# Weighted sum of the expert rows on VectorE: four operations over four token tiles in place of eight over one

## What is computed

```python
x = x + 0.5 * ffn(layernorm(x))
x = x + attn(layernorm(x))
x = x + 0.5 * ffn(layernorm(x))

def ffn(x):                     # 8 experts, the 2 best of each token
    gates = softmax(x @ gate_w)
    top_v, top_i = top_k(gates, 2)
    top_v = top_v / sum(top_v)
    eo = gelu(x @ fc_w[e]) @ proj_w[e]          # for every expert e
    return sum over the two choices c of top_v[c] * eo[top_i[c]]
```

## Time and profile before

| what | us |
|---|---|
| median of 3 runs | 1348.94 |
| range of the runs | 1347.59 to 1349.1 |
| profiled execution | 1347.8 |
| its span in the profile | 1346.0 |
| VectorE busy | 840.0 (62%) |
| GpSimd busy | 650.5 (48%) |
| TensorE busy | 1029.9 (77%) |
| busy time of L824, 96 instructions | 40.8 |

### The profile page before, as it was taken

The page is one execution under the profiler, slowest core; times in us unless marked ns, Lnnn a source line. Parts: engine busy times, 40 slices in busy tenths (PEclk is TensorE's granted clock), DMA queues, the critical chain, the costliest instruction groups (busy, mean ns, idle before and its releaser), DMA issues.

```text
span 1346.0 us, 23815 instructions
## 1 busy us (share of the span) xinstructions
PE 1029.9 (77%) x7084; PEld 899.3 (67%) x7084; DVE 840.0 (62%) x2514; ACT 722.3 (54%) x1804; POOL 650.5 (48%) x473
## 2 busy tenths in 40 slices
PE   1428788750899999999999999999999706878870
PEld 1427777740787778878778778877887606777770
DVE  4662222227888887888888888888887493222226
ACT  1102222211888888888889889888898201222220
POOL 1146777743353444434444444444444044777772
PEclk9988999985999999999999999999999658999995
DMA  7896555541000000000000000000000203555545
GB/s 207 116 167 197 147 152 156 151 132 54 1 2 1 1 1 1 2 1 1 1 1 1 1 1 1 1 1 1 1 1 1 63 0 115 154 149 153 152 111 187
DMA packets 61065, 87.13 MB, mean 65 GB/s; under 512 B 8019, under 2 KB 32598, under 8 KB 60944
## 3 DMA queue, kind: packets, MB, share of 16 engines
q1 hardware_dynamic: 51200, 66.08, 18.9%
q0 software_dynamic: 9744, 19.56, 4.9%
HBM read 65.67 MB, written 20.97 MB: 64 GB/s over the span
## 4 chain that ended last, share of the span: by engine, by line
PE 47%; DVE 22%; DMA 10%; issue 9%; POOL 9%; ACT 1%; DVEq 1%; another core or an unknown queue 0%; SPq 0%; POOLq 0%; ACTq 0%
PE bank L1046 8%; DMA xr<-xn_dram,gidx 7%; PE bank L1020 6%; DVE qst L857 6%; PE bank L1036 6%; PE bank L1037 5%; POOL y_dram L504 5%; PE bank L1058 4%; PE bank L1056 4%; DVE prob L879 3%; PE bank L976 3%; POOL xr L498 3%; PE bank L986 3%; DVE x_sb L824 2%; DVE in_tile L753 2%
## 5 line engine op out<-in xcount | busy, mean ns | idle before, releaser
L536 POOL TENSOR_TENSOR prob<-prob,rsum 128x512 f32<-128x512 f32 (+3 forms) x128 | 296.1, 2321 | 381.5 <-DVE rsum L886 381.5
L600 ACT ACTIVATE prob<-prob,negmax 128x384 f32<-128x384 f32 (+3 forms) x512 | 283.2, 556 | 25.9 <-DVE negmax L879 24.2
L879 DVE CUSTOM_DVE_ANT_0 prob<-bank,bias_tab 128x384 f32<-128x384 f32 (+3 forms) x512 | 243.1, 489 | 70.8 <-PE bank L1037 60.2
L578 ACT ACTIVATE hT<-bank 128x512 f32<-128x512 f32 x144 | 86.0, 597 | 372.6 <-PE bank L976 372.6
L891 DVE TENSOR_TENSOR pl<-bank,ph 128x512 fp32r<-128x512 f32 x320 | 219.9, 687 | 26.0 <-ACT ph L609 22.4
L1036 PE MATMUL bank<-kst,qst 128*128 128x256 f32 (+2 forms) x512 | 182.6, 371 | 23.3 <-DVE qst L857 21.0
L609 ACT ACTIVATE ph<-bank 128x512 fp32r<-128x512 f32 x320 | 188.8, 590 | 19.6 <-PE bank L1046 17.3
L1046 PE MATMUL bank<-ident,prob 128*128 128x128 f32 x1280 | 193.7, 274 | 0.7 <-POOL prob L536 0.6
L1046 PEld LDWEIGHTS bank<-ident,prob 128*128 128x128 f32 x1280 | 156.8, 140 | 48.1 <-POOL prob L536 10.2
L815 DVE COPY yo<-bank 128x128 f32<-128x128 f32 x144 | 42.0, 292 | 214.1 <-PE bank L986 209.9
L498 POOL DMA_INDIRECT xr<-xn_dram,gidx x144 | 140.1, 973 | 72.8 <-issue 31.1
(11 more groups left out here) (152 smaller groups left out, 1366.9 us busy)
## 6 DMA issues: line engine op xcount, KB each, us to landing
w1t<-L_ffn_fc_w SPq DMA_DIRECT2D x144, 256.0 KB
in_tile<-y_dram SPq DMA_DIRECT2D x16, 512.0 KB, 4.3
bias_dram<-hg SPq DMA_DIRECT2D x1, 5120.0 KB, 52.9
xn_dram<-in_tile SPq DMA_DIRECT2D x8, 512.0 KB, 2.9
bias_tab<-bias_dram SPq DMA_DIRECT2D x1, 4096.0 KB, 13.0
xr<-xn_dram,gidx POOLq DMA_INDIRECT x144
y_dram<-yo,sidx POOLq DMA_INDIRECT x144
x_sb<-L_attn_x SPq DMA_DIRECT2D x4, 512.0 KB, 7.9
```

The source lines that it names most:

```text
L536: g.tensor_tensor(out=pv, in0=pv, in1=rsum[:, n % 4, :].unsqueeze(2).to_broadcast([P, HG, (n % QT + 1) * P]), op=ALU.mult).then_inc(norm_d ...
L600: a.activation(prob[n % QT][:, h, :], prob[n % QT][:, h, :], ACT.Exp, scale=-1.0, bias=negmax[:, (HG * n + h) % 8:(HG * n + h) % 8 + 1], a ...
L879: v.tensor_tensor_reduce(out=prob[n % QT][:, h, :], in0=front[:, 0:w], in1=bias_tab[:, HG * (n // QT) + h, SEQ - w:SEQ], scale=-1.0, scala ...
```

## The change

The loop is unrolled, and a group is now four `tensor_tensor` instructions of 128x512 in place of eight `scalar_tensor_tensor` of 128x128. The first two multiply the rows of both choices in their buffer by the weights, which are read with a step of zero along the features. The third adds the first product to x, the fourth the second. The fourth waits for the third and for the second multiplication. It raises `combined` by four at once, which is what SyncE's waits count on.

```diff
-                with dve.Fori(0, TILES // 16) as i:
+                for i in range(TILES // 16):
                     for u in range(3):
-                        dve.wait_ge(y2_in[u], (i + (r * (TILES // 16) + 1)) * 16)
+                        done = (r * (TILES // 16) + i) * 9 + 3 * u
+                        own = slice(i * 16 + u * 4, i * 16 + u * 4 + 4)
+                        dve.wait_ge(y2_in[u], (r * (TILES // 16) + i + 1) * 16)
                         for c, w in ((0, gw1), (1, gw2)):
-                            for q in range(4):
-                                t = i * 16 + (u * 4 + q)
-                                xt = x_sb[:, ds(t, 1), :].rearrange("p a d -> p (a d)")
-                                v.scalar_tensor_tensor(out=xt, in0=yc[:, u, q, c * D:(c + 1) * D], scalar=w[:, ds(t, 1)],
-                                                       in1=xt, op0=ALU.mult, op1=ALU.add).then_inc(comb1 if c == 0 else combined, 1)
-                            if c == 0:
-                                dve.wait_ge(comb1, i * 12 + (r * (TILES * 3 // 4) + (u + 1) * 4))
+                            part = yc[:, u, :, c * D:(c + 1) * D]
+                            v.tensor_tensor(part, part, w[:, own].unsqueeze(2).to_broadcast([P, 4, D]), ALU.mult).then_inc(comb1, 1)
+                        dve.wait_ge(comb1, done + 1)
+                        v.tensor_tensor(x_sb[:, own, :], x_sb[:, own, :], yc[:, u, :, 0:D], ALU.add).then_inc(comb1, 1)
+                        dve.wait_ge(comb1, done + 3)
+                        v.tensor_tensor(x_sb[:, own, :], x_sb[:, own, :], yc[:, u, :, D:2 * D], ALU.add).then_inc(combined, 4)
```

## The result

The changed kernel takes 1353.36 us (median of 9 runs), the kernel before 1348.87 in the same comparison. The ratio is 1.0033 with a 95% interval of 1.0018 to 1.0047: it is slower by 4.5 us, 2.4 to 6.3. One of the nine runs took 1597.42 us at a granted clock of 0.655, and the ratio leaves it out. The forecast was 1351.3 with a range of 1348.2 to 1354.2. The time lies in the range, but the ratio is above the limit of 0.2% (2.7 us) under which I had put the larger chance.

A forecast was written before the change was run, and what follows sets the result against it. VectorE and its hold-ups by GpSimd were taken to bound both combine stages, about 21 us each. First stage +1.6 and second +0.8 gave +2.4 us on 1348.94: 1351.3 us, range 1348.2 to 1354.2.

The forecast's parts named there:

- An undisturbed group costs 0.28 us more: Combine stages: a VectorE group not meeting GpSimd's work takes 2.59 us in place of 2.31.
- Rival B: Combine stages: each wide VectorE operation must end before the next starts, giving 1353.9 us; chance 0.18.
- Turns of whole operations: Combine stages: VectorE and GpSimd alternate one whole operation each; GpSimd's lengthen from 1.07 and 1.26 to 1.4 and 1.6 us.
- Rival A: Combine stages: GpSimd isn't delayed, its chain stays 4.8 us, both stages stay within 0.3 us: 1348.9; chance 0.18.
- rival C: Combine stages: the new form doesn't collide and both engines run side by side, faster at 1344.3 us; chance 0.07.
- First stage, +1.6: First combine stage: GpSimd's second chain ends last, so the statistics start at 320.65 in place of 319.09.
- Second stage, +0.8: Second combine stage: GpSimd's chain ends at 1341.0, so the second output transfer goes later; +0.9, taken as +0.8 us.
- The sum: Both combine stages together: +2.4 us on the kernel before's median of 1348.94.
- the outer part of the forecast's bounds: Share of the forecast's own chance, 0.22 of 0.57, put beyond the 0.2% (2.7 us) limit; its bounds were +0.8 and +4.6.
- a GpSimd start that overlaps nothing: Upper bound, both stages: GpSimd's start can't overlap VectorE's turn, six or seven turns cost 0.17 more each; total +4.6 us.
- The loop's branch and register work: Combine loop: unrolling removes this work, but no gap at the loop's turn is on record, so worth 0.
- My sign that something outside the sum was at work: Attention, between the stages: a length change of over 1 us would make the sum wrong for an outside reason.

The follow-up runs named there:

- E5: Changed kernel with both products written to PSUM, so the additions read only one SBUF input; ratio 0.9989 to the kernel before, 1.5 us faster.
- E6: Changed kernel with products and weights both in PSUM, so no VectorE operation of the stage has two SBUF inputs; ratio 0.9968, 4.3 us faster than before.
- E8: Kernel before, unrolled, with a group's running sum in PSUM, so the second four operations read one SBUF input; ratio 0.9982, 2.4 us faster.
- E1: The changed kernel run again without edit, on another chip; ratio 1.0026 to the kernel before, 3.7 us on 1431.96.
- E2: Kernel before with only the loop unrolled, its eight 128x128 operations a group kept; ratio 0.9985, 2.1 us faster.
- E3: Kernel before with GpSimd's operations cut from 128 features to 1, leaving out most of its sums; ratio 0.9893, 15.3 us faster.
- E4: Changed kernel with GpSimd's operations cut from 128 features to 1; ratio 0.9926 to the kernel before, 10.6 us faster.
- E9: Changed kernel with GpSimd's rows brought first; ratio 1.0011 to the kernel before, 1.6 us slower, interval reaching to no change.
- E12: As E6, with GpSimd's rows brought first; ratio 0.9918 to the kernel before, 11.7 us faster.

## Why the prediction was right, step by step

**An undisturbed group costs 0.28 us more: right.** Forecast 2.59 us, measured 2.60 to 2.61. Two small errors cancel in it: the spacing is 0.60 and not 0.62, and the step over the wait 0.79 and not 0.73. The duration was forecast at 0.69 and is 0.69. The price came from other shapes of the same operation. Rival B, with 0.73 between starts, falls.

**Turns of whole operations: right.** I had 1.4 and 1.6 us for L514 and L519; they measure 1.42 and 1.59. A turn of each engine together takes 1.46 us with a multiplication and 1.67 with an addition, where I had 1.40 and 1.62. VectorE's longest operations are 1.75, above the 1.4 to 1.6 that I had named. Rival A (GpSimd isn't delayed) falls with that, rival C (side by side) with VectorE's operations above 0.8, of 1.34 to 1.75. E5, E6 and E8 show the condition: it is the second input in SBUF. The rule of the Trainium skill, "SBUF — State Buffer", section "Who interferes with whom", says the same; by that rule, the trace agrees.

**First stage, +1.6: measured +1.8 in the changed kernel, +1.9 in E1** (25.0, 26.8, 26.9). Counted from VectorE's first operation, as I had it, the stage takes 22.99 and 23.11 us where I had 22.6. The sum was nearly right, one link was not. I had the refill of GpSimd's buffer released by VectorE's third group. In the profile it was released by GpSimd's own first chain, 2.8 us behind VectorE's group. GpSimd's rows landed later in this execution, 6.2 us behind VectorE's start and not 4.8, and its chain then met VectorE's fourth group too. In E1, where they landed 5.1 us behind it, the refill stood behind VectorE's group as forecast, and the stage is as long. That GpSimd would end the stage came true in E1, where VectorE waits 1.22 us for it; in the first profile VectorE's last operation ends it, held up until GpSimd was done.

**Second stage, +0.8: mis-sized; it measures +2.0** (31.6 to 33.6). This is the term that brought the result over 0.2%. Two things are in it. GpSimd's last chain starts 17.2 us behind VectorE's first operation where I had 16.9, and it lasts 6.1 and not 5.7: in my sequence GpSimd won the first turn there, and in the run it lost it, to an operation that VectorE had started 0.22 us before.

```profile
1340.73 0.68 DVE L824 TENSOR_TENSOR in_tile<-in_tile,gw 128x512 f32<-128x512 f32 x1
```

```profile
1340.95 1.36 POOL L514 TENSOR_TENSOR in_tile<-in_tile,gw 128x512 f32<-128x512 f32 x1 [7.04 <-DMA in_tile<-y_dram]
```

That makes 0.7 us. And I let the end follow the last output transfer (1340.10 before) and even took 0.1 us off, as it would share the engines with no neighbour. The end follows GpSimd's last operation: it lies 5.9 us behind the last output's issue before the change and 6.5 in the changed kernel (1347.12). That is another 0.7. VectorE's start, 0.24 us sooner behind the first transfer than before, takes some back. What the end follows is the matter of the last section.

**The sum** was +2.4. The two stages give +3.8, the measurement +4.5 and, again, +3.7. I had put B and the outer part of the forecast's bounds, 0.40 together, on slower by over 0.2%, and 0.53 on within. The first came. That the time still lay in the range owes something to luck. The room above the forecast was there for B and for a GpSimd start that overlaps nothing. B fell, and the turns were only 0.05 us longer than forecast. What filled the room was the second stage, which I had mis-sized by 1.2 us; neither bound was about its end.

The loop's branch and register work, which I had put at nothing, do cost something: E2 is faster than the kernel before by 0.7 us in the stages and 2.1 by the ratio. The forecast for the new form did not need that term, since its groups were built up from single operations. My sign that something outside the sum was at work, attention longer by over 1 us, was not met (729.5 us before and after).

## What to carry to other kernels

Before making operations wider, count the elements that they stream. Here one fused pass became two. The fixed part between two starts went from 48 x 0.13 to 24 x 0.07 us a stage, 4.6 us less, and the elements from 6144 to 12288, 6.4 us more. The difference of 1.8 is what E3 and E4 show (14.02 and 15.88).

Where VectorE and GpSimd work at once, look at how many of VectorE's inputs lie in SBUF. Putting the second one in PSUM took away the hold-up of both engines, with the same additions and multiplications. What it gives depends on the bound underneath; here 4.3 us became 11.7 only when GpSimd's rows were brought first.

## What the runs showed of the hardware that I had not expected

The program ends a fixed time after GpSimd's last operation, when that comes late enough. GpSimd's last instruction in the changed kernel:

```profile
1345.50 1.59 POOL L519 TENSOR_TENSOR x_sb<-x_sb,in_tile 128x512 f32<-128x512 f32 x1
```

It ends at 1347.09, and the span at 1353.6: 6.5 us. Before the change it ended at 1339.51 and the span at 1346.0, also 6.5:

```profile
1338.25 1.26 POOL L519 TENSOR_TENSOR x_sb<-x_sb,in_tile 128x512 f32<-128x512 f32 x1
```

In E1 it is 1429.29 and 1435.8, in E3 1407.67 and 1414.2, in E6 1338.41 and 1344.9: 6.5 each. It is not the landing of the last output. In E3 GpSimd was done 0.3 us before the last output was even issued (1408.01), and the span still ends 6.5 us behind GpSimd. SyncE's waits at the end of E1 (us in total, times, longest) show that landing as 1.9 us and then 4.0 us more for TensorE's sequencer at the end of the program; in E9, where GpSimd is done early, the second wait is 0.2:

```profile
SPq L81 <- PEq L81: 4.0, 1, 4.0
SPq L81 <- DMA out<-x_sb: 1.9, 1, 1.9
```

```profile
SPq L81 <- DMA out<-x_sb: 2.3, 1, 2.3
SPq L81 <- PEq L81: 0.2, 1, 0.2
```

In E9 GpSimd ends at 1423.51, and the span at 1432.7, 3.2 us behind the last issue of an output (1429.46). So the end is the later of two: GpSimd's last operation and 6.5 us, or the last output's issue and 3.2. This fits all fourteen profiles within 0.1 us. What fills the 6.5 us isn't shown by these traces, and no run was made for it. It means that the kernel before did not end with the landing of its outputs, as I had written, but with GpSimd. The profile's chain of waits puts that end on VectorE's last operation (until 1339.66), but VectorE is done 6.3 us before the end of the span there and 7.6 us in the changed kernel (1345.97), where GpSimd has 6.5 in both. It also means that part of what E9 to E12 gained is there: in E12 the two come out together (1412.70 + 6.5 = 1419.2, and the span is 1419.4).
